# Expert weights in a fused attention and expert layer: sigmoids kept from selection, a product on GpSimd, fewer VectorE operations

## What is computed

```python
x = x + tanh(g_xattn) * xattn(layernorm(x), ctx)      # 2 x 1024 tokens of 256; 64 context rows, 16 heads of 64
y = layernorm(x)
scores = sigmoid(y @ W_gate_router)                    # 8 experts
_, sel = top_k(scores + expert_bias, 2)
top = take_along_axis(scores, sel, axis=1)
top = top / (top.sum(-1, keepdims=True) + 1e-20)
shared = (silu(y @ Wg_s) * (y @ Wu_s)) @ Wd_s
routed = sum over the two chosen experts of top * ((silu(y @ Wg[e]) * (y @ Wu[e])) @ Wd[e])
x = x + tanh(g_ffn) * (shared + routed)
```

## Time and profile before

| | us |
|---|---|
| median of 3 runs | 305.51 |
| lowest and highest | 304.73, 306.84 |
| span of the profiled execution | 304.1 |

### The profile page before, as it was taken

One profiled execution on the slowest core, in us unless ns is written; L12 is line 12 of the kernel. 1 busy time (PEld: TensorE's weight loads), 2 busy tenths in 40 slices (PEclk: granted clock), 3 DMA queues, 4 the chain that ended last, 5 costly groups with the idle time before them and its releaser, 6 DMA issues.

```text
span 304.1 us, 6562 instructions
## 1 busy us (share of the span) xinstructions
PE 274.8 (90%) x1746; PEld 246.3 (81%) x1747; DVE 239.4 (79%) x691; ACT 160.7 (53%) x414; POOL 172.6 (57%) x234
## 2 busy tenths in 40 slices
PE   2899989999999999999996668988799999999994
PEld 1788767998897898999886657877699899999883
DVE  0489989899899789899989565479877777777684
ACT  1452475656666566564453433654455555566731
POOL 8012225777758886897855876648544344444430
PEclk9999999999999999999999999999999999999999
DMA  6999994123359999923121122323343434446796
GB/s 185 361 288 314 306 293 140 41 77 100 103 167 302 312 286 318 270 69 106 35 70 56 59 81 90 105 56 86 90 118 111 123 96 122 121 114 167 249 325 232
DMA packets 45006, 49.74 MB, mean 164 GB/s; under 512 B 3928, under 2 KB 41650, under 8 KB 44978
## 3 DMA queue, kind: packets, MB, share of 16 engines
q1 hardware_dynamic: 39938, 39.37, 45.5%
q0 software_dynamic: 3408, 8.46, 8.1%
q10 hardware_dynamic: 1632, 1.57, 1.5%
HBM read 21.67 MB, written 28.64 MB: 165 GB/s over the span
## 4 chain that ended last, share of the span: by engine, by line
PE 60%; DVE 24%; issue 8%; ACT 4%; DMA 2%; SPq 1%; ACTq 0%; DVEq 0%
PE bank L1401 7%; PE bank L1403 6%; PE bank L1402 5%; PE scores_ps L1401 5%; PE scores_ps L1403 4%; PE scores_ps L1402 4%; DVE row_max L1146 3%; DVE probs L1152 3%; DVE row_sum L1136 3%; PE bank L1347 3%; DVE pT_lo L1129 3%; PE scores_ps L1438 2%; PE bank L1598 2%; DMA Wq_sb<-in_L_xattn_Wq_dram 2%; PE bank L1438 2%
## 5 line engine op out<-in xcount | busy, mean ns | idle before, releaser
L699 POOL DMA_INDIRECT routed_dram<-probs,sct_idx x39 | 38.1, 977 | 49.3 <-ACT probs L911 46.8
L649 POOL TENSOR_TENSOR probs<-probs,row_inv 128x1024 f32<-128x1024 f32 x16 | 30.5, 1909 | 26.4 <-DVE row_inv L1140 26.3
L613 POOL DMA_INDIRECT rows_dram<-xn,slot_i x32 | 32.0, 1000 | 14.0 <-issue 10.5
L1401 PE MATMUL bank<-AB_hi,pT_hi 128*128 128x256 f32 x128 | 37.0, 289 | 2.4 <-DVE pT_lo L1129 2.4
L1403 PE MATMUL bank<-AB_hi,pT_lo 128*128 128x256 f32 x128 | 35.8, 279 | 0.0
L1402 PE MATMUL bank<-AB_lo,pT_hi 128*128 128x256 f32 x128 | 35.7, 279 | 0.0
L768 ACT ACTIVATE probs<-probs 128x1024 f32<-128x1024 f32 x16 | 17.0, 1061 | 29.5 <-DVE probs L1152 25.4
L1401 PE MATMUL scores_ps<-AB_hi,xnT_hi 128*128 128x512 f32 x64 | 27.0, 421 | 2.5 <-DVE xnT_lo L1122 2.3
L1401 PEld LDWEIGHTS bank<-AB_hi,pT_hi 128*128 128x128 f32 x128 | 24.1, 188 | 3.0 <-issue 2.9
L1403 PE MATMUL scores_ps<-AB_hi,xnT_lo 128*128 128x512 f32 x64 | 25.3, 395 | 0.0
L1402 PE MATMUL scores_ps<-AB_lo,xnT_hi 128*128 128x512 f32 x64 | 25.3, 395 | 0.0
(11 more groups left out here) (248 smaller groups left out, 876.6 us busy)
## 6 DMA issues: line engine op xcount, KB each, us to landing
rows_dram<-pad_rows SPq DMA_DIRECT2D x10, 1040.0 KB, 16.5
rows_dram<-pad_rows SPq DMA_DIRECT2D x8, 780.0 KB, 12.2
AB_free<-routed_dram SPq DMA_DIRECT2D x8, 512.0 KB, 6.4
probs<-rows_dram SPq DMA_DIRECT2D x30, 130.0 KB
raw_buf<-in_L_ffn_Wg_dram SPq DMA_DIRECT2D x8, 192.0 KB, 2.5
raw_buf<-in_L_ffn_Wu_dram SPq DMA_DIRECT2D x8, 192.0 KB, 2.6
out_dram<-x_sb ACTq DMA_DIRECT2D x6, 256.0 KB, 2.9
pT_hi<-rows_dram SPq DMA_DIRECT2D x9, 130.0 KB
```

Source lines behind the costliest of these rows:

```text
L613: nc.gpsimd.indirect_dma_start(rows_dram[:, :], bass.IndirectOffsetOnAxis(ap=slot_i[:, t, k:k + 1], axis=0), xn2[:, t % KEEP, :], None).th ...
L649: nc.gpsimd.tensor_tensor(pr, pr, row_inv[:, :].unsqueeze(2).to_broadcast([P, H, KV]), ALU.mult).then_inc(norm_done, 1)
L699: nc.gpsimd.indirect_dma_start(routed_dram[:, :], bass.IndirectOffsetOnAxis(ap=sct_idx[(k - 2) % (2 * RING)][:, 0:1], axis=0), y_sb[ks][:, ...
L1401: nc.tensor.matmul(out_ap, a_hi, b_hi, start=first, stop=False)
```

## The change

- `choose` writes its sigmoids to `score` in SBUF, for the batch's tiles, instead of to PSUM. `scores_again` is gone.
- GpSimd multiplies `hot` by `score` before its adds in the expert loop, at j = -1, after it has waited for the last batch's row numbers, and signals `hot_scored`.
- In slot 4 VectorE waits for that and reduces. In slot 5 one `scalar_tensor_tensor` makes (a + eps) + b of the two picked scores, and a reciprocal follows. In slot 6 one `scalar_tensor_tensor` makes (picked x tanh gate) x inverse.

```diff
@@ expert_step on GpSimd
+                if isinstance(j, int) and j == -1:
+                    pool.wait_ge(slot_done, len(BATCHES))
+                    nc.gpsimd.tensor_tensor(hot_val[:, :, :, :], hot[:, :, :, :],
+                                            score[:, :, :].unsqueeze(2).to_broadcast([P, T, TOPK, E]),
+                                            ALU.mult).then_inc(hot_scored, 1)
@@ choose
-                part = score_at[:, 0:g * E].rearrange("p (t e) -> p t e", e=E)
+                part = score[:, a:z, :]
@@ VectorE, weights
-            def scores_again():
-
-                chain(nc.vector.tensor_scalar(score[:, :, :], exp_neg[:, :, :], 1.0, None, ALU.add))
-                chain(nc.vector.reciprocal(score[:, :, :], score[:, :, :]))
-
             def pick():
 
-                chain(nc.vector.tensor_tensor(hot_val[:, :, :, :], hot[:, :, :, :],
-                                              score[:, :, :].unsqueeze(2).to_broadcast([P, T, TOPK, E]), ALU.mult))
+                dve.wait_ge(hot_scored, 1)
                 chain(nc.vector.tensor_reduce(picked[:, :, :], hot_val[:, :, :, :], AX_X, ALU.add))
 
+            def divisor():
+
+                chain(nc.vector.scalar_tensor_tensor(out=den[:, :], in0=picked[:, :, 0], scalar=ROUTE_EPS, in1=picked[:, :, 1],
+                                                     op0=ALU.add, op1=ALU.add))
+                chain(nc.vector.reciprocal(den[:, :], den[:, :]))
+
             def weigh():
 
-                chain(nc.vector.tensor_tensor(den[:, :], picked[:, :, 0], picked[:, :, 1], ALU.add))
-                chain(nc.vector.tensor_scalar(den[:, :], den[:, :], ROUTE_EPS, None, ALU.add))
-                chain(nc.vector.reciprocal(den[:, :], den[:, :]))
-                chain(nc.vector.tensor_scalar(den[:, :], den[:, :], tgate[:, 1:2], None, ALU.mult))
-                nc.vector.tensor_tensor(weight[:, :, :], picked[:, :, :], den[:, :].unsqueeze(2).to_broadcast([P, T, TOPK]),
-                                        ALU.mult).then_inc(weights_done, 1)
+                nc.vector.scalar_tensor_tensor(out=weight[:, :, :], in0=picked[:, :, :], scalar=tgate[:, 1:2],
+                                               in1=den[:, :].unsqueeze(2).to_broadcast([P, T, TOPK]),
+                                               op0=ALU.mult, op1=ALU.mult).then_inc(weights_done, 1)
@@ expert_step on VectorE
                 if isinstance(j, int) and j == 4:
-                    scores_again()
+                    pick()
                 if isinstance(j, int) and j == 5:
-                    pick()
+                    divisor()
```

More of the change, by code:

```diff
@@ L211, in flamingo_layer @@
         rank_at, count_ps = route[:, 0:4 * E], route[:, 32:32 + E]
-        score_at, e_at = route[:, 64:64 + 4 * E], route[:, 96:96 + 4 * TOPK]
+        e_at = route[:, 96:96 + 4 * TOPK]
         part_ps, ctiles_ps, tiles_ps, end_ps = [route[:, c:c + E] for c in (112, 120, 128, 136)]
@@ L275, in flamingo_layer @@
         weights_done = sem("weights_done")
+        hot_scored = sem("hot_scored")
         diag_done = sem("diag_done")
```

## The result

| | median, us | runs | ratio to before, 95% interval |
|---|---|---|---|
| before | 305.44 (304.06 to 307.13) | 20 | |
| after | 303.88 (301.60 to 306.79) | 20 | 0.9943 (0.9919 to 0.9968) |

The change makes the kernel 0.6% faster, some 1.6 us, where 0.7 us slower had been forecast. That is inside the range and within the 1%, but with the sign turned. The ratio leaves out three executions of after that were over 1.5% above its fastest, and the first profile of after, 306.79 us, is one of the three. Two later comparisons of the same pair stand under the experiments.

A forecast was written before the change was run, and what follows sets the result against it. TensorE (60% of the span on the chain of waits) and VectorE (24%) take turns. Selection's +3.75 us less the expert loop's 3.0 gave +0.75: span 304.9, median 306.2 us, range 302.5 to 308.5.

The forecast's parts named there:

- h(4) to h(8): Expert loop, between the first up-projection matmuls of slots 4 and 8: gain of 3.5 us, between 2.8 and 4.3.
- Slot 6: Expert loop: one VectorE operation of 32 elements waits for GpSimd's add, 0.33 us behind the beat; with no wait nothing.
- slot 5: Expert loop: the new two-input VectorE operation waits for GpSimd's first add, 0.50 us behind the beat.
- The 0.5 us for slot 1: Expert loop: GpSimd's product pushes its fourth add into VectorE's tile counting and index operations; cost 0 to 0.75 us.
- batch 3: Selection: the bias addition waits 1.5 us behind GpSimd's normalization, L1026's 0.27 us wait goes away; net 1.25 us lost.
- then the addition falls into GpSimd's power operation: Selection, batch 0: the bias addition waits behind GpSimd's 0.57 us power operation; batch total 0.65 to 1.05, taken as 0.9.
- Batches 5 and 6: Selection, among GpSimd's indirect DMAs: VectorE waits of 0.15 us in batch 5 and 0.3 us in batch 6.
- b0 to h(0): From batch 0's tensor_scalar in selection to slot 0's first up-projection matmul: selection's waits lose 3.75 us, between 2.4 and 5.0.
- B: Rival: selection is not held, its small operations slip in; only the expert loop's gain stays, 302.5 us; chance 0.13.
- A: The forecast itself, selection's waits against the expert loop's gain: 306.2 us, own range 303.6 to 308.5; chance 0.65.
- C: Rival: GpSimd retakes the port between its instructions, VectorE waits for whole runs in selection; +5.05, 310.5 us; chance 0.08.
- D: Rival: new operations in slots 5, 6 and 1 wait longest for adds; the loop gains 2.0, 307.3 us; chance 0.14.

The follow-up runs named there:

- again: Second profiles, from unchanged copies of the same two kernels: before measured 305.31 us (1.001), after 302.52 us (0.9937).
- sel_only: Before with one edit: selection writes its sigmoids to SBUF, the rest as before; 307.59 us, 1.0102 to before.
- adds_early: After with 1 + exp and the bias in PSUM, and all twelve GpSimd adds in slot 0; 303.89 us, 0.9992 to before.
- old_weigh: After with before's five weight operations in slot 6 and none in slot 5; 306.56 us, 1.0033 to before.
- best: After with selection's second operands in PSUM and GpSimd's twelve adds in slots 32 to 37; 305.26 us, 1.0005 to before.
- late_adds: After with GpSimd's twelve adds in slots 32 to 37 instead of 0 to 5; 309.49 us, 1.0119 to before.

## Why the prediction was right or wrong

**Expert loop: the mechanism and the size were right, a term beside it was not.** For h(4) to h(8) I had 3.5 us, 2.8 to 4.3; measured 3.77, 3.45 and 3.76 in the three profiles of after. Slot 4 cost nothing. Slot 6 was held as I wrote in two of the three (L1253 0.70 and 0.59), and free in the second profile (0.25). In slot 5 the size fits (0.43 against 0.50), the instruction does not: the index operation ahead of it was held, inside a DMA with an add behind it, and L1247 came too late to meet the add. That the size fits is in part luck. The trace before had this wait already: L1309 takes 0.80 at 210.39, and VectorE comes to the head of slot 5 at 211.73, h(5) + 1.51, where I used slot 4's lag of 1.17 for every slot. The 0.5 us for slot 1 was mis-sized. I put the fourth add into the tile counting, and VectorE comes to it 0.39 after that add ended. I had read where the adds stand from one profile: there they end 2.40 us after h(0) (201.27 and 198.87), in the second profile of before 1.33 after (199.04 and 197.71), and in after, product included, 1.85. The loop's gain is 3.5 in the cleanest pair (both "again"), not 3.0.

**Selection: the places were right, the sum was too large.** The tensor_scalar of batches 0 and 2 cost 0.5 and 0.4 (forecast 0.65 and 0.5), batch 3 about 1.1 (1.25). The step that failed is "then the addition falls into GpSimd's power operation": that was 0.25 of batch 0, 0.3 of batch 1 and 0.35 of batch 2, 0.9 us in all, and it cost nothing. I carried the wait from GpSimd operations of 256 and 1024 elements, for which I had rows, to one of a single element, for which I had none. Zero was its lower bound in the range (2.4), but the forecast itself took it near the middle. Batches 5 and 6 (0.45) were not held either (0.17 each). b0 to h(0) lost 2.2 us against 3.75 forecast. (The terms' upper bounds add up to 5.3, not 5.0; nothing hangs on it.)

**The sum.** With the measured terms: + 2.2 - 3.5 = -1.3 us, near the 1.6, 2.3 and 1.0 of the medians. Both mis-sized terms leaned the same way (1.5 in selection, 0.5 in slot 1), 2 us together, and the forecast was +0.75. The sign turned on them. The profiles end 2.8 us apart (303.5 and 300.7, both "again"); the rest of that is ahead of b0 (0.9) and in the tail (0.7), where the change does nothing that I can name. The rivals: B's time (302.5) is closer than A's (306.2), but B as a whole is wrong, since sel_only lost 1.0% and the waits are in every profile; only the six additions other than batch 3's slipped in as B has it (0.17 to 0.22). C did not come in selection; adds_early shows its mechanism, a turn for GpSimd after each VectorE operation, where GpSimd has a train of adds. D did not come: the loop gained 3.5, not 2.0. A loop that gains about as little is old_weigh's, 1.6 us.

**The clock** was in none of my sums. In all seven profiles with batch 3's wait TensorE idles 0.50 to 0.52 us and then 1.5 us around that batch's end; in the seven without it (before, and all with batch 3 in PSUM) it idles there once, for 1.14 to 1.16. The granted clock falls there in five of the seven with the wait and in none of the seven without; two of the latter (best, adds_early) have a fall some 20 us later, at batches 5 and 6, that costs 0.8 to 0.9. The fall at batch 3 costs 2.1 us in the first profile of after (20.58 against 18.44) and in late_adds, and 1.0 to 1.1 in the other three. Over all runs it counts for less, since before falls somewhere too: a mean clock of 0.995 or below is seen in 24 of 44 runs of after and 31 of 93 of before. With the 1.1 to 1.7 us between the medians of such runs and of the others, it is an estimate of 0.2 to 0.4 us on after's median. It is a loose one: in the first group of experiments such runs are 5 of 12 for after and 14 of 23 for before. That the wait causes the fall is a pattern of 14 profiles, and I have no run that lengthens that idle alone; it stays open.

## What to carry to other kernels

Before moving a small VectorE operand from PSUM to SBUF, look at what GpSimd runs at that moment: beside GpSimd operations of 256 elements or more the operation paid the rest of the running instruction, each time, and where one of its two inputs could be kept in PSUM, the wait went (2.1 to 2.7 us here). Leave GpSimd's own work where someone has slack, not at the end of a loop that the next stage waits on. In a sum of small waits, work out the total once more with every term that has no row of its own at nothing: if the sign turns, as it does here, the sign is not known. And read the lag of a stage from that stage's own rows, and from two profiles where there are two.

## What the runs showed of the hardware

- GpSimd's power operation (128x1, 0.54 to 0.57 us) does not hold a VectorE addition with two SBUF inputs: 0.18 us inside it, in batches 0, 1 and 2 of after and of every other profile with such inputs. Its tensor_tensor operations of 256 to 1024 elements do hold VectorE operations with two SBUF inputs (L1253 0.70 in an add, the bias addition 1.62 in the normalization). Whether the kind or the size of the GpSimd operation makes the difference is not shown.
- A small VectorE operation of the expert loop (index, sum or weight, with operands in SBUF) that starts inside one of GpSimd's indirect DMA records is held only where an add stands directly behind the DMA. Over the 14 profiles 397 start inside a DMA with no add directly behind, and none is held; 39 start inside one with an add directly behind, and 29 are held, nearly all until 0.1 us after the DMA's record ends: 0.83 at 212.73 in after. The ten that are free started in the DMA's first 0.26 us: 0.21 at 215.33. This is a pattern read from traces; why it is so is open.
- Selection's tensor_scalar from SBUF to SBUF (128x24) takes 0.11 us with nothing of GpSimd's beside it (158.00 in after), where the one to PSUM takes 0.17; that gives back 0.06 of batch 3's wait. In the batches where it starts inside a small GpSimd operation or an indirect DMA it takes 0.17 even when it is not held (batches 1, 4, 5 and 6 of after). The reciprocal takes 0.30 in SBUF and 0.32 in PSUM (128x24), the bias addition 0.18 with its first input in either.
